# Expert tiles made of two 128-row halves with an expert each: fifteen tiles of 88 narrow up products in place of eighteen tiles of 44 wide ones

## What is computed

```python
x = x + _layernorm(attn(_layernorm(x)))          # 16 heads of 16, causal
xt = _layernorm(x).reshape(-1, 256)              # 4096 tokens
topk_w, topk_idx = jax.lax.top_k(xt @ Ws + bs, 2)
topk_w = softmax(topk_w)
g = jnp.einsum('td,edf->tef', xt, Wg)            # 8 experts, f = 688
u = jnp.einsum('td,edf->tef', xt, Wu)
y = jnp.einsum('tef,efd->ted', silu(g) * u, Wd)
x = x + _layernorm(jnp.einsum('ted,te->td', y, combine))
```

## Time and profile before

| | |
|---|---|
| median of 3 runs | 888.35 us (885.34 to 891.23) |
| time of the profiled execution | 890.5 us |
| its span, first instruction to last | 888.7 us |
| TensorE busy / its weight loads | 718.2 us (81%) / 471.2 us |
| VectorE, ScalarE, GpSimd busy | 635.0, 536.3, 434.0 us |
| stage 3, from its first up matmul to the last of `down` | 678.15 to 851.5 us |

### The profile page before, as it was taken

One profiled execution on the slowest core, in us unless ns is written; L12 is line 12 of the kernel. 1 busy time (PEld: TensorE's weight loads), 2 busy tenths in 40 slices (PEclk: granted clock), 3 DMA queues, 4 the chain that ended last, 5 costly groups with the idle time before them and its releaser, 6 DMA issues. The chain is left out here.

```text
span 888.7 us, 22060 instructions
## 1 busy us (share of the span) xinstructions
PE 718.2 (81%) x6822; PEld 471.2 (53%) x6823; DVE 635.0 (71%) x2034; ACT 536.3 (60%) x1086; POOL 434.0 (49%) x515
## 2 busy tenths in 40 slices
PE   3476787778788899979998998889885999999930
PEld 1144444445443355545554564567773878778720
DVE  5777898889877988887897778467551556556545
ACT  4688875867656676756765674665642444344427
POOL 3563432644534556774675467577352233242228
PEclk9889997989985799999988997899996999999975
DMA  6435232463332101221112111223335233233248
GB/s 192 136 118 153 82 113 71 126 194 116 112 130 63 43 14 26 50 48 26 26 28 53 19 32 34 41 40 57 50 86 137 37 44 46 36 47 42 30 113 291
DMA packets 72812, 68.91 MB, mean 78 GB/s; under 512 B 6800, under 2 KB 66320, under 8 KB 72720
## 3 DMA queue, kind: packets, MB, share of 16 engines
q1 hardware_dynamic: 59440, 53.23, 19.7%
q0 software_dynamic: 13280, 14.49, 11.6%
HBM read 34.04 MB, written 31.29 MB: 74 GB/s over the span
## 5 line engine op out<-in xcount | busy, mean ns | idle before, releaser
L944 ACT ACTIVATE pT<-bank 128x512 f16<-128x512 f32 (+1 forms) x384 | 200.3, 534 | 100.1 <-PE bank L1521 98.7
L728 POOL TENSOR_SCALAR_AFFINE_SELECT pT<-pT 128x512 f16<-128x512 f16 x128 | 88.2, 734 | 144.7 <-ACT pT L944 144.4
L1087 DVE TENSOR_REDUCE nmax<-bank 128x1 f16<-128x384 f32 (+2 forms) x216 | 126.1, 597 | 34.7 <-PE bank L1510 33.3
L1944 POOL DMA_INDIRECT expert_rows<-y_sb,dest x36 | 56.0, 1554 | 120.1 <-DVE y_sb L2063 114.6
L1100 DVE CUSTOM_DVE_ANT_0 unused<-bank,mask 128x384 f16<-128x384 f32 (+2 forms) x224 | 103.6, 483 | 14.4 <-PE bank L1499 12.8
L2138 PE MATMUL bank<-xT,gu_part 128*128 128x256 f16 (+1 forms) x792 | 95.9, 280 | 2.6 <-issue 1.7
L1614 PE MATMUL bank<-tile_xT,gu_part 128*128 128x256 f16 (+1 forms) x616 | 90.9, 289 | 8.5 <-DVE stage L1284 8.4
L2138 PEld LDWEIGHTS bank<-xT,gu_part 128*128 (+1 forms) x792 | 78.5, 102 | 19.0 <-issue 4.2
L1552 PEld LDWEIGHTS bank<-va,pT 128*128 128x128 f16 x1280 | 55.4, 99 | 51.1 <-issue 27.8
L1552 PE MATMUL bank<-va,pT 128*128 128x17 f16 x1280 | 68.0, 174 | 15.8 <-POOL pT L728 15.8
L162 POOL DMA_INDIRECT dispatch_rows<-rows,slot x64 | 66.9, 1046 | 21.5 <-issue 16.7
(11 more groups left out here) (218 smaller groups left out, 1618.6 us busy)
## 6 DMA issues: line engine op xcount, KB each, us to landing
expert_rows<-tile_in SPq DMA_DIRECT2D x8, 1024.0 KB, 6.2
stage<-wg SPq DMA_DIRECT2D x8, 688.0 KB, 4.2
stage<-wu SPq DMA_DIRECT2D x8, 688.0 KB, 4.2
stage<-wd SPq DMA_DIRECT2D x8, 640.0 KB, 4.3
gu_part<-expert_rows SPq DMA_DIRECT2D x16, 256.0 KB, 5.7
out<-gu_part SPq DMA_DIRECT2D x16, 256.0 KB, 2.9
tile_in<-dispatch_rows SPq DMA_DIRECT2D x21, 130.0 KB, 2.2
rows<-dispatch_rows SPq DMA_DIRECT2D x18, 130.0 KB, 2.2
```

The costliest lines, as they stand in the source:

```text
L728: last = gp.affine_select(out=diagonal, in_=diagonal, compare_op=ALU.is_ge, fill=0.0, base=0, pattern=[[0, J], [1, P]], channel_multiplier=-1)
L944: sc.activation(pT[:, lo:hi], ST_BANK[i % 2][:, 0:hi - lo], ACT.Exp, scale=1.0 / INV_SCALE).then_inc(p_ready, 1)
L1087: v.tensor_reduce(columns, S_BANK[i % 2][:, 0:n * len(heads)].rearrange("p (j n) -> p j n", n=n), AX.X, ALU.max, negate=True).then_inc(s_m ...
```

## The change

A tile stays 256 rows, but its two halves of 128 rows come from two places and each has an expert of its own. A region's tail is rounded up to 128 rows rather than 256, and the static number of later tiles falls from 18 to 15 (30 halves). The 21 early tiles, the attention and stage 4 stay as they are.

- The constants, the table (30 columns rather than 18), its planning in `later` (steps of 128) and the pads (one row per partition for each expert rather than two) follow the new step. Two scratch tiles of the planning move from `xnT` to `kT`.
- SyncE loads each tile with two table reads and two DMAs of 128 rows; the waits on `xin_in` count two.
- `up`: each product over 256 rows becomes two over 128 rows, with the same stationary size, one for each half's weights.
- `down`: still 34 matmuls of the same shape, but with an address per half.
- `expert_of` reads two numbers.

```diff
+LATER_ROWS = TOP * B * T - EARLY_TILES * TS
+LATER_TILES = -(-((LATER_ROWS + E * (P - 1)) // P) // 2)
+HALVES = LATER_TILES * TS // P
...
                 def load(h, j):
-                    row = sp.value_load(table[0:1, 0, bass.ds(2 * h + j, 1)], min_val=0, max_val=ROWS - TS)
-                    sp.dma_start(xin[j][:, :, :], rows_of(xs_dram, row)).then_inc(xin_in[j], 16)
+                    for t in range(TT):
+                        row = sp.value_load(table[0:1, 0, bass.ds(2 * TT * h + (TT * j + t), 1)], min_val=0, max_val=ROWS - P)
+                        sp.dma_start(xin[j][:, t, :], xs_dram[bass.ds(row, P), :]).then_inc(xin_in[j], 16)
...
-                            for s in range(2 * KD):
-                                k, part = s // 2, s % 2
-                                last = mm(dst[0:width, :], gu_part[part][:, bass.ds(col + (k * GU + at), width)],
-                                          xT[j][:, k, :], start=(s == 0), stop=(s == 2 * KD - 1))
+                            for t in range(TT):
+                                for s in range(2 * KD):
+                                    k, part = s // 2, s % 2
+                                    last = mm(dst[0:width, P * t:P * (t + 1)],
+                                              gu_part[part][:, bass.ds(col[t] + (k * GU + at), width)],
+                                              xT[j][:, k, P * t:P * (t + 1)], start=(s == 0), stop=(s == 2 * KD - 1))
...
-                    return pe.value_load(table[0:1, 1, bass.ds(i, 1)], min_val=0, max_val=E - 1)
+                    return [pe.value_load(table[0:1, 1, bass.ds(TT * i + t, 1)], min_val=0, max_val=E - 1) for t in range(TT)]
...
-                                          wd_part[w][0:rows, bass.ds(col + c * D, D)],
+                                          wd_part[w][0:rows, bass.ds(col[t] + c * D, D)],
```

More of the change, by code:

```diff
@@ L45 @@
 REGION = B * T + TS
[L46 to L49, removed]
 W = D + 4
 FIRST_TILE = 4 * G + 2
-M_MAX = B * T // TS
+M_MAX = B * T // P
 WOVEN = G * B - FIRST_TILE
@@ L133, in build @@
             "tile_y_ready": sem("tile_y_ready"),
-            "table": sb(outer, "later_table", [P, 2, LATER_TILES], U32),
+            "table": sb(outer, "later_table", [P, 2, HALVES], U32),
             "table_ready": sem("table_ready"),
@@ L225, in attention @@
         gap_y = qT[:, 0:2, :].rearrange("p g t -> p (g t)").bitcast(F32).rearrange("p (t d) -> p t d", d=D)
-        pads = pT[:, 0:E * (TS // P) * W].bitcast(F32).rearrange("p (e t w) -> p e t w", t=TS // P, w=W // 2)
-        scratch = xnT[:, :, :].rearrange("p k t -> p (k t)").bitcast(F32)
+        pads = pT[:, 0:E * W].bitcast(F32).rearrange("p (e w) -> p e w", w=W // 2)
+        scratch = kT[:, :, :].rearrange("p g t -> p (g t)").bitcast(F32)
         over, later_past, later_mine = [scratch[:, at:at + n] for at, n in (
-            (0, E * M_MAX), (E * M_MAX, LATER_TILES * (E + 1)), (E * M_MAX + LATER_TILES * (E + 1), LATER_TILES * (E + 1)))]
+            (0, E * M_MAX), (E * M_MAX, HALVES * (E + 1)), (E * M_MAX + HALVES * (E + 1), HALVES * (E + 1)))]
         over = over.rearrange("p (e m) -> p e m", e=E)
@@ L232, in attention @@
         small = xn[:, :, :].rearrange("p t d -> p (t d)").bitcast(F32)
[L233 to L237, removed]
+        iota_m, iota_i, iota9, one9 = small[:, 0:M_MAX], small[:, 32:32 + HALVES], small[:, 64:73], small[:, 80:89]
+        count, later_tiles, later_cum, later_start = small[:, 96:104], small[:, 112:121], small[:, 128:137], small[:, 144:153]
+        later_own, later_row, later_ownc = [small[:, at:at + HALVES] for at in (160, 192, 224)]
+        pad_ids = small[:, 256:256 + E]
+        fill_u = small[:, 272:272 + E].bitcast(U32)
         unused = sb(stack, "unused", [P, 2, T], F16)
@@ L644, in _ @@
                     row = sp.value_load(fill_u[0:1, e:e + 1], min_val=0, max_val=ROWS - TS)
-                    sp.dma_start(xs_dram[bass.ds(row, TS), :].rearrange("(p t) w -> p (t w)", p=P),
-                                 pads[:, e, :, :].rearrange("p t w -> p (t w)")).then_inc(padded, 16)
+                    sp.dma_start(xs_dram[bass.ds(row, P), :], pads[:, e, :]).then_inc(padded, 16)
                 sp.wait_ge(x1_out, 16 * B + 16)
@@ L653, in _ @@
                 for j in range(2):
-                    row = sp.value_load(keep["table"][0:1, 0, j:j + 1], min_val=0, max_val=ROWS - TS)
-                    sp.dma_start(first_later_rows(keep, j), xs_dram[bass.ds(row, TS), :].rearrange("(t p) d -> p t d", p=P)
-                                 ).then_inc(keep["xin_in"][j], 16)
+                    for t in range(TS // P):
+                        at = TS // P * j + t
+                        row = sp.value_load(keep["table"][0:1, 0, at:at + 1], min_val=0, max_val=ROWS - P)
+                        sp.dma_start(first_later_rows(keep, j)[:, t, :], xs_dram[bass.ds(row, P), :]
+                                     ).then_inc(keep["xin_in"][j], 16)
             @block.gpsimd
@@ L1046, in _ @@
                 v.memset(nmax[:, 1, :, :], 0.0).then_inc(pv_mm, NF)
-                HALVES = (range(QT // 2), range(QT // 2, QT))
+                TILE_HALVES = (range(QT // 2), range(QT // 2, QT))
                 def norm_stats(src, half):
-                    for t in HALVES[half]:
+                    for t in TILE_HALVES[half]:
                         last = v.bn_stats(stats[:, t, :], src[:, t, :])
@@ L1399, in later @@
                 def later():
-                    fill, following, n_ = keep["fill"], keep["next"], LATER_TILES
+                    fill, following, n_ = keep["fill"], keep["next"], HALVES
                     lch.link(v.tensor_tensor(count, fill[:, :], following[:, 0:E], ALU.subtract))
@@ L1418, in later @@
                     lch.link(v.reduce_sum(later_row, later_mine, AX.X))
-                    lch.link(v.scalar_tensor_tensor(later_row, iota_i, float(TS), later_row, ALU.mult, ALU.add))
+                    lch.link(v.scalar_tensor_tensor(later_row, iota_i, float(P), later_row, ALU.mult, ALU.add))
                     lch.link(v.tensor_scalar(later_ownc, later_own, float(E - 1), None, ALU.min))
@@ L1446, in _ @@
                         lch.link(v.memset(pads, 0.0))
-                        lch.link(v.tensor_copy(pads.bitcast(U32)[:, :, :, D // 2], pad_ids))
+                        lch.link(v.tensor_copy(pads.bitcast(U32)[:, :, D // 2], pad_ids))
                     if m == 4:
@@ L2170, in tile @@
                     i = 2 * h + j
-                    col_gu, col_d = expert * (KD * GU), expert * (FC * D)
+                    col_gu, col_d = [e * (KD * GU) for e in expert], [e * (FC * D) for e in expert]
                     pe.wait_ge(xT_ready, i + 1)
```

26 lines of the change are left out of this document (13 added, 13 removed).

## The result

The changed kernel takes 962.45 us (median of 4 runs, 956.86 to 962.9), the one before 887.9 us beside it (4 runs, 885.34 to 891.23): a ratio of 1.0795, 95% interval 1.0753 to 1.0837. It is 7.95% slower, and the forecast was 963 us. The profiled execution took 962.12 us, with a span of 960.3 us against 888.7.

What follows compares the result with a forecast made beforehand. TensorE's sequencer, 122.5 ns per register instruction, was taken to pace up products after the change: fifteen 16.0 us tiles, loop ends, first pass and readings add 74.2 us to 888.35 us, said as 963 us, range 944 to 986 us.

Steps and rivals of the forecast that it cites:

- The speed of the sequencer, 122.5 ns: TensorE's up products: each register instruction with its weight load and matmul takes 122.5 ns, 10.8 us a tile for 88.
- From up to down, and down: Within a stage 3 tile: 0.4 us from up to `down`, unchanged, then 4.8 us of `down` with two table readings.
- a full queue: In `down` before the change: about 0.5 us in which the sequencer found the queue full, gone after it.
- A tile: Stage 3: 10.8 + 0.4 + 4.8 = 16.0 us a tile against 9.3 us before; fifteen are 240 us.
- Loop ends: Ends of TensorE's loop iterations in stage 3: three, at 2.0 us extra each, 6 us.
- First pass: Stage 3 code on its first run seems slower: 2 us added for four tiles and the three behind the loop.
- The sum: Stage 3 takes 247.3 us plus 0.3 us, against 173.4 us before: +74.2 us, so 963 us in all.
- The array's rate decides: Up products: register instructions overlap once matmuls are short, 4.7 to 6.6 us a tile; middle 869 us; chance 0.05.
- Part of the way: Up products: the 256-column matmul holds back part of the register step; 100 ns each, tile 14.0 us, 933 us; chance 0.08.
- Clock falls in part or wholly: Stage 3: TensorE's granted clock drops from full after the change; chance 0.12.
- the half-time clock case: Stage 3: the case of a low TensorE clock that sets the range's upper end, 986 us.
- The change doesn't do what it says: Stage 3: a tile count or addresses that don't follow; the forecaster saw no way for it.

Runs made afterwards that it cites:

- Experiment 2: Kernel before, each up product split into two of 128 rows that share one register address (88 narrow matmuls, 44 register instructions a tile): 891.66 us, ratio 1.0014.
- experiment 9: Changed kernel, second half's up products over the upper 128 input values reuse the first half's expert and registers, 66 register instructions for 88 matmuls: 920.38 us.
- experiment 10: Changed kernel, all the second half's up products reuse the first half's expert and registers, 44 register instructions for 88 matmuls: 886.88 us.
- Experiment 7: Changed kernel with TensorE's fifteen tiles written out, no loop: 949.77 us, ratio 1.0644 to the kernel before.
- experiment 1: Changed kernel with fixed weight addresses in its up products, so no register instruction on the up line: 877.25 us.
- experiment 4: Changed kernel with fixed weight addresses in its down products, up as changed: 933.9 us.
- experiment 6: Kernel before with fixed weight addresses in its up products: 890.0 us beside 891.47 us, ratio 0.9984.

## Why the prediction was right

**The speed of the sequencer, 122.5 ns.** Right: 121 ns between up matmuls, 10.52 us on the chain where 10.8 were forecast. What told it ahead was that the register instructions kept their step in the earlier trace rows while the matmuls' step changed. Experiment 2 shows that it is the register instruction, experiments 9 and 10 that it counts one by one, at 117 ns.

**From up to down, and down.** Forecast 0.4 + 4.8 us, measured 0.39 + 4.98 us. The two readings of the table in a row make the 0.83 us in which TensorE is idle inside `down`; they hold the sequencer for 1.6 us (775.08 to 776.71 us), where I had put 1.4. One reading of mine was wrong: the 0.5 us that I took from the earlier trace rows for a full queue are a wait. The register instructions stop from 725.2 to 725.8 us, and go on 0.05 us after VectorE's second remainder (L2050) ends at 725.76 us. It does fall away after the change, as I had it, but because the remainder is done before `down` begins (772.73 us in the tile shown).

**A tile.** 16.0 forecast, 15.89 measured in the loop. Behind the loop it is shorter, 15.6 us (893.22 to 908.80 us on the chain), with the table read at fixed places; this I hadn't counted.

**Loop ends.** Forecast 6 us for three. On the chain TensorE stands idle 1.88, 1.86 and, where the loop is left, 1.12 us: 4.9 us.

**First pass.** Forecast 2 us in all. In the first iteration the pairs are slower:

```profile
L2139 PEldq FUSED_REGOPS  x44: 46/46/46, 727.7 to 738.4; - x44
```

10.7 us over 43 = 249 ns a pair against 244 in the second iteration. Right in sign and about in size. Experiment 7, in which every tile's code runs once, has 249 to 252 ns in all fifteen tiles; why code is slower on its first run was not tried.

**The sum.** The stage ran from 678.15 us, where its first up product began before, to 923.5 us: 245.4 us where 247.6 were forecast and 173.4 stood before. Ahead of it nothing moved (the first transposes are at 676.8 us in both), and SyncE's two further loads before the block's end cost nothing: they end at 671.5 us, 2.2 us later than before. Behind it 36.8 us remain against 37.2 us. That the total agrees to within 1 us is partly luck: between the profiled executions lie 71.6 us where I forecast 74.2, with the tiles and the loop ends each a little too dear, and the medians, 74.6 us apart, carry a few us of scatter.

**The rivals.** *The array's rate decides*, 869 us: fell. Its price was right, though, 56 ns a matmul in experiments 1 and 2, within the 4.7 to 6.6 us a tile that I gave it; but with a register instruction ahead of each matmul that rate is not reached. *Part of the way*, 933 us: fell with the slope of experiments 9 and 10. *Clock falls in part or wholly*: it did in part, in three short stretches (6.8, 3.4 and 3.4 us), each behind a loop end; apart from them it was 1.00 from 684.2 us on. In experiment 7, which has the same up products and no loop, it stayed at 1.00 throughout. And where it fell the up matmuls kept their 122 ns, and it had come back before `down` began (752.5 us in the tile whose `down` begins at 757.42 us). The chance of 0.12 and the upper end of the range, the half-time clock case, were my estimates: no run shows a stage with the clock low half the time, the mean in this one was 0.97. *The change doesn't do what it says*: the trace has 1320 up matmuls, 15 times 88.

**What was off.** In experiments 4 and 6: the lead that the sequencer gains during `down` (2.2 us a tile, not 1.6), and the claim in my reading of before that TensorE alone bounds the stage. The chain over ScalarE, VectorE and the reading of the table set its 9.27 us a tile, 0.1 to 0.3 us above what the matmuls need. It didn't matter for this change, since the slower up product leaves ScalarE 151 us of waiting.

## What to carry to other kernels

Count the register instructions where addresses depend on data: each takes some 120 ns of TensorE's sequencer here, with one wide, one narrow or two narrow matmuls behind it, so a matmul of 256 columns (109 ns) nearly hides one, and one of 128 columns (56 ns) only half. Before cutting work into finer pieces with an address each, compare the steps of the sequencer's rows with those of the matmuls in a stretch with an empty queue: a busy share of PE near 100% says nothing about which of the two paces it (159.7 of 162 us in the stage before, 222.6 of 239 us in the changed one, where the sequencer paced the up products). Where several matmuls can share one computed address, most of the time comes back (887 us with 44 instructions, 877 with none). In the paired layout they can't, since the two halves have different experts; the kernel before is the order that shares. And where the profile names a releaser, compare it with the wait in the code: here a copy on ScalarE was named, and the sequencer was reading a table.

## What the runs showed that I had not expected

- The granted clock fell to 0.50 behind a TensorE idle time of less than 2 us at each loop end, while up matmuls 122 ns apart, with no loop between the tiles, left it at 1.00 in experiment 7, from 684 us to the stage's end. In the kernel before, where a loop end leaves TensorE idle for 0.65 us at most, it stayed at 1.00 too, in 684 to 846 us.
- The low clock was free where the sequencer was the bound: 122 ns between up matmuls at 0.50, 121 ns at 1.00. It cost some 2.4 us in one tile of experiment 10, where the matmuls were the bound.
- The loop around TensorE's tiles costs 5 us in the kernel before (0.9938) and some 11 to 13 us in the changed one.
- Taking the register instructions out of the up products of the kernel before gives next to nothing, because a chain over ScalarE, VectorE and the sequencer's reading of the table is as long.
